# A mixture-of-experts tower: the gate rides in the routed row, the expert pass multiplies by it, and the gathers add rows into their target

## What is computed

```python
h = tok(x)                                       # softmax attention over patches
h = h + attn(layernorm(h), ...)                  # causal linear attention
h = h + ffn_moe(layernorm(h), ...)               # 8 experts, top 2
h = h + l1_attn(layernorm(h), ...)               # L1-normalised linear attention
h = h + bitlinear_ffn(layernorm(h), ...)         # quantised feed-forward

def ffn_moe(x, ...):
    routing = softmax(gelu(x @ w1 + b1) @ w2 + b2)
    topv, topi = top_k(routing, 2)
    sparse = one_hot(topi) * topv, summed over the two
    sparse = sparse / (sum(sparse) + 1e-8)       # the two gates of a token
    z = gelu(x @ down_w[e] + down_b[e])
    moe = sum over e of sparse[e] * (z @ up_w[e])
    return layer_norm(x + moe, gamma, beta)
```

## Time and profile before

| | |
|---|---|
| runs, us | 2739.93, 2738.08, 2753.07 |
| span of the profiled execution, us | 2748.1 |
| busy us: PE, DVE, ACT, POOL | 2290.8, 1996.1, 1551.7, 1004.0 |
| indirect transfers on POOL | 224 scatters, 241.3 us; 224 gathers, 229.3 us |
| first instruction of stage 3, of stage 4, us from the start | 1441.3, 1797.2 |

### The profile page before, as it was taken

One profiled execution on the slowest core, in us unless ns is written; L12 is line 12 of the kernel. 1 busy time (PEld: TensorE's weight loads), 2 busy tenths in 40 slices (PEclk: granted clock), 3 DMA queues, 4 the chain that ended last, 5 costly groups with the idle time before them and its releaser, 6 DMA issues. The chain is left out here.

```text
span 2748.1 us, 45420 instructions
## 1 busy us (share of the span) xinstructions
PE 2290.8 (83%) x14046; PEld 1660.5 (60%) x14047; DVE 1996.1 (73%) x5437; ACT 1551.7 (56%) x2693; POOL 1004.0 (37%) x1024
## 2 busy tenths in 40 slices
PE   8999999999996999999937999926778794666665
PEld 4444444444444888888827999925576684444443
DVE  5777777777763899999944444447698877899986
ACT  2444444444444788888734565536566551777776
POOL 1100100100000266566652444478787720344433
PEclk9999999999998999999958999957688886777776
DMA  2000000000002011111136777721111100000000
GB/s 57 0 18 13 0 18 13 0 9 1 0 0 90 16 53 51 51 52 52 51 111 221 257 252 258 238 77 50 46 48 43 46 9 22 21 26 21 26 26 26
DMA packets 69143, 162.81 MB, mean 59 GB/s; under 512 B 12977, under 2 KB 32342, under 8 KB 68702
## 3 DMA queue, kind: packets, MB, share of 16 engines
q1 hardware_dynamic: 39426, 94.27, 10.4%
q0 software_dynamic: 21504, 44.99, 5.8%
q10 hardware_dynamic: 8064, 21.68, 2.6%
HBM read 63.98 MB, written 63.88 MB: 47 GB/s over the span
## 5 line engine op out<-in xcount | busy, mean ns | idle before, releaser
L211 ACT ACTIVATE prob<-pscore 128x896 f32<-128x896 f32 x336 | 308.0, 917 | 423.9 <-PE pscore L293 423.9
L418 DVE TENSOR_REDUCE pmax<-ppre 112x1 f32<-112x512 f32 x656 | 424.5, 686 | 162.0 <-PE ppre L260 161.9
L307 PE MATMUL pout<-prob,xkey 128*64 128x448 f32 x1344 | 328.3, 567 | 0.4 <-ACT prob L211 0.4
L260 PE MATMUL ppre<-xh,yh 49*112 49x512 f32 x656 | 291.4, 446 | 7.8 <-DVE pmax L418 4.2
L723 POOL DMA_INDIRECT rows_in<-xr,idx x224 | 241.3, 1077 | 127.1 <-DVE idx L1249 69.5
L193 POOL CAST yh<-ynext 113x448 fp32r<-113x448 f32 x28 | 17.2, 614 | 667.5 <-DVE pmax L418 639.4
L260 PEld LDWEIGHTS ppre<-xh,yh 49*112 49x112 f32 x656 | 112.7, 172 | 239.8 <-issue 103.5
L1708 POOL DMA_INDIRECT yg<-rows_out,place x224 | 229.3, 1024 | 62.4 <-issue 62.1
L293 PE MATMUL pscore<-yh,xh 49*128 49x448 f32 x700 | 241.1, 422 | 0.4 <-DVE yh L438 0.4
L2223 POOL TENSOR_TENSOR yg<-y,gout 112x512 f32<-112x512 f32 x112 | 141.1, 1270 | 258.6 <-DVE y L2456 258.6
L1558 POOL TENSOR_TENSOR zl<-z,zh 128x448 fp32r<-128x448 f32 x126 | 144.5, 1147 | 218.3 <-ACT zh L1524 208.8
(11 more groups left out here) (388 smaller groups left out, 6558.0 us busy)
## 6 DMA issues: line engine op xcount, KB each, us to landing
wd<-down SPq DMA_DIRECT2D x63, 512.0 KB, 3.0
xb<-rows_in SPq DMA_DIRECT2D x63, 448.0 KB, 3.6
rows_out<-yb ACTq DMA_DIRECT2D x63, 336.0 KB, 3.1
out<-ho SPq DMA_DIRECT2D x28, 336.0 KB, 2.8
rows_in<-zero SPq DMA_DIRECT2D x15, 448.0 KB
rows_in<-xr,idx POOLq DMA_INDIRECT x224
yg<-rows_out,place POOLq DMA_INDIRECT x224
xkey<-in_xkey SPq DMA_DIRECT2D x4, 800.0 KB, 6.6
```

The costliest lines, as they stand in the source:

```text
L211: nc.scalar.activation(prob[j % 3][:, :, :], pscore[j % 2][:, :, 0:CH], ACT.Exp).then_inc(exped, 1)
L260: pe.matmul(out[:, :], yh1[rows, q * T:(q + 1) * T], xh[b % 2][rows, block * 512:(block + 1) * 512], start=True, stop=True, tile_position= ...
L307: mm = pe.matmul(pout[i * LO:(i + 1) * LO, 0:CH], xkey[b % 2][:, 2 * j + i, :], prob[j % 3][:, i, :], start=(j == 0), stop=(i == 1 and j = ...
L418: nc.vector.reduce_max(pmax[:, q, 2 * block + half:2 * block + half + 1], bank(u, depth), AX.X).then_inc(pre_max, 1)
```

## The change

Five things are moved or replaced.

- The rows of `rows_in`, `xr3`, `xb3` and the zero block grow from 256 to 260 floats (1024 to 1040 bytes). Column 256 carries the gate; columns 256 to 259 are cleared once. The table `gate3` of all tokens goes; two small buffers for one group stay.
- Stage 2: `share(r)` moves from the end of DVE's round to right behind `places(r)`. POOL's `scatter(r, k)` sends first the four sets with k = 0 and then, behind `factor`, the four with k = 1; ahead of each four it copies the gate of that k into column 256 of `xr3`, and ahead of the second copy it waits until the first four transfers have landed.
- Stage 3: a new `take_gate(t)` on DVE copies column 256 of the loaded rows to a small buffer, behind `take_y(t-2)`; `take_y` multiplies by it, four instructions of 192 columns in place of two copies of 384. `load(t)` on SP now also waits for the gate of tile t-2 (`gate_out`).
- Stage 4: the eight multiply-adds of `add_experts` go. The gathers target `acc3` itself and add to it (`compute_op=ALU.add`), first the four sets with k = 0, ahead of `factor`, then the four with k = 1, behind it and behind a wait for the first four. `acc3` has four buffers in place of three, ACT fills it one step earlier, and `yg3` goes.
- Waits that fed the removed instructions go (`half_out`, `acc_out`), others come (`gate_out`, `gate_in`, `xa_out` on POOL).

```diff
+ROW = 260
...
-            def scatter(r, tiles):
-
-                if 0 in tiles:
-                    pool.wait_ge(R["idx_out"], r + 1)
-                for q in tiles:
-                    for k in range(2):
-                        nc.gpsimd.indirect_dma_start(
-                            rows_in, bass.IndirectOffsetOnAxis(ap=idx[r % G3][:, 2 * q + k:2 * q + k + 1], axis=0),
-                            xr[r % G3][:, q, :], None).then_inc(scattered[r % G3], 16)
+            def scatter(r, k):
+
+                pool.wait_ge(R["gate_out"], r + 1)
+                pool.wait_ge(R["xr_ready"], r + 1)
+                if k:
+                    pool.wait_ge(scattered[r % G3], 16 * (2 * TPC * (r // G3) + TPC))
+                nc.gpsimd.tensor_copy(xr[r % G3][:, :, 256:257], gate[r % 2][:, :, k:k + 1]).then_inc(R["gate_in"], 1)
+                pool.wait_ge(R["gate_in"], 2 * r + k + 1)
+                pool.wait_ge(R["idx_out"], r + 1)
+                for q in range(TPC):
+                    nc.gpsimd.indirect_dma_start(
+                        rows_in, bass.IndirectOffsetOnAxis(ap=idx[r % G3][:, 2 * q + k:2 * q + k + 1], axis=0),
+                        xr[r % G3][:, q, :], None).then_inc(scattered[r % G3], 16)
...
                 if here(g - 3):
                     places(g - 3)
+                    share(g - 3)
...
-                if here(g - 3):
-                    share(g - 3)
...
                     sp.wait_ge(S["xtr_mm"], t - 1)
+                    sp.wait_ge(S["gate_out"], t - 1)
...
+            def take_gate(t, i):
+
+                dve.wait_ge(S["xtr_mm"], t + 1)
+                if not isinstance(t, int) or t >= 2:
+                    dve.wait_ge(S["y_out"], 2 * t - 2)
+                nc.vector.tensor_copy(gate[i][:], xb[i][:, :, 256:257]).then_inc(S["gate_out"], 1)
+
             def take_y(t, i, n):
 
+                dve.wait_ge(S["gate_out"], t + 1)
...
-                    nc.vector.tensor_copy(yb[i][:, 2 * pair:2 * pair + 2, :].rearrange("p q d -> p (q d)"),
-                                          py[i][:, pair, 0:2 * D]).then_inc(S["y_out"], 1)
+                    for q in (2 * pair, 2 * pair + 1):
+                        ts = nc.vector.tensor_scalar(yb[i][:, q, :], py[i][:, pair, (q % 2) * D:(q % 2 + 1) * D],
+                                                     gate[i][:, q, :], None, ALU.mult)
+                    ts.then_inc(S["y_out"], 1)
...
+            def gather_rows(g, k):
+
+                if k:
+                    pool.wait_ge(gathered[g % 2], 16 * (2 * TPC * (g // 2) + TPC))
+                else:
+                    pool.wait_ge(S["xa_out"], g + 1)
+                for q in range(TPC):
+                    c = g * 2 * TPC + 2 * q + k
+                    nc.gpsimd.indirect_dma_start(acc[g % 4][:, q, :], None, rows_out,
+                                                 bass.IndirectOffsetOnAxis(ap=place[:, c:c + 1], axis=0),
+                                                 compute_op=ALU.add).then_inc(gathered[g % 2], 16)
...
                 if here(s + 4):
-                    gather_rows(s + 4, (0, 1, 2))
+                    gather_rows(s + 4, 0)
                 if here(s + 3):
                     factor(s + 3)
                 if here(s + 4):
-                    gather_rows(s + 4, (3,))
+                    gather_rows(s + 4, 1)
...
-                for k in range(2):
-                    for q in range(TPC):
-                        st = nc.vector.scalar_tensor_tensor(acc[g % 3][:, q, :], yg[g % 2][:, q, k, :],
-                                                            gate[:, g * TPC + q, k:k + 1], acc[g % 3][:, q, :],
-                                                            ALU.mult, ALU.add)
```

More of the change, by code:

```diff
@@ L551, in _, with attend_route_phase @@
             inverse_root(nc, dve, link, rstd[:], var[:], root[:], dif[:])
-def attend_route_phase(nc, ins, h, bns, mean, rstd, minus, eye, held, gate, slot, shift, tile_e, tile_r, down,
+def attend_route_phase(nc, ins, h, bns, mean, rstd, minus, eye, held, slot, shift, tile_e, tile_r, down,
                        rows_in, scattered):
@@ L606, in attend_route_phase @@
         steps = sb("steps3", [T, 64])
-        zero = sb("zero3", [T, TPC * 256])
+        zero = sb("zero3", [T, TPC * ROW])
         agg3 = sb("agg3r", [T, TPC, 2])
         veps3 = sb("veps3r", [T, TPC])
-        xr = [sb(f"xr3_{i}", [T, TPC, 256]) for i in range(G3)]
+        xr = [sb(f"xr3_{i}", [T, TPC, ROW]) for i in range(G3)]
+        gate = [sb(f"gate3_{i}", [T, TPC, 2]) for i in range(2)]
         xrT = sb("xrT3", [KC, 2, CH])
@@ L694, in _ @@
                 pool.wait_ge(S["w_ready"], n + 1)
-            for n, (buf, value) in enumerate(((r1[KC:KC + 1], 1.0), (zero[:], 0.0))):
+            for n, (buf, value) in enumerate(((r1[KC:KC + 1], 1.0), (zero[:], 0.0), *((x[:, :, 256:ROW], 0.0) for x in xr))):
                 nc.gpsimd.memset(buf, value).then_inc(R["w_ready"], 1)
@@ L1233, in share @@
                 link(nc.vector.reciprocal(both[:], both[:]))
-                link(nc.vector.tensor_tensor(gate[:, r * TPC:(r + 1) * TPC, :], top[:, :, 0:2],
-                                             both[:].broadcast_to([T, TPC, 2]), ALU.mult))
+                if r >= 2:
+                    dve.wait_ge(R["gate_in"], 2 * r - 2)
+                nc.vector.tensor_tensor(gate[r % 2][:], top[:, :, 0:2], both[:].broadcast_to([T, TPC, 2]),
+                                        ALU.mult).then_inc(R["gate_out"], 1)
             def take_rank(r):
@@ L1358, in expert_phases @@
             route_sems = []
-            attend_route_phase(nc, ins, h, bns, mean, rstd, minus, eye, route_sems, gate, slot, shift, tile_e, tile_r,
+            attend_route_phase(nc, ins, h, bns, mean, rstd, minus, eye, route_sems, slot, shift, tile_e, tile_r,
                                down, rows_in, scattered)
@@ L1362, in expert_phases @@
                        held + route_sems)
-        linear_attention_phase(nc, ins, h, bns, rstd, minus, eye, gate, place, rows_out)
+        linear_attention_phase(nc, ins, h, bns, rstd, minus, eye, place, rows_out)
 def tile_phase(nc, ins, eye, down, slot, place, shift, tile_e, tile_r, rows_in, rows_out, held):
@@ L1372, in tile_phase @@
         downb = sb("downb", [128, 2 * E])
-        xb = [sb(f"xb3_{i}", [T, TPC, 256]) for i in range(2)]
+        xb = [sb(f"xb3_{i}", [T, TPC, ROW]) for i in range(2)]
+        gate = [sb(f"gate3b_{i}", [T, TPC, 1]) for i in range(2)]
         xth = [sb(f"xth3b_{i}", [128, 2, CH], F32R) for i in range(2)]
@@ L1603, in tile @@
                     take_y(t - 1, 1 - i, n + i - 1)
+                if not last:
+                    take_gate(t + 1, 1 - i)
                 if isinstance(t, int) and t == 2:
@@ L1613, in _ @@
             take_low(0, 0)
+            take_gate(0, 0)
             split_low(0)
@@ L1617, in _, with linear_attention_phase @@
             take_y(NTILE - 1, (NTILE - 1) % 2, (NTILE - 1) // 2)
-def linear_attention_phase(nc, ins, h, bns, rstd, minus, eye, gate, place, rows_out):
+def linear_attention_phase(nc, ins, h, bns, rstd, minus, eye, place, rows_out):
     RB = D - 128
@@ L1632, in linear_attention_phase @@
         mhalf = sb("mhalf_3", [T, TPC])
-        yg = [sb(f"yg3_{i}", [T, TPC, 2, D]) for i in range(2)]
-        acc = [sb(f"acc3_{i}", [T, TPC, D]) for i in range(3)]
+        acc = [sb(f"acc3_{i}", [T, TPC, D]) for i in range(4)]
         yf = sb("yf3", [T, TPC, D])
@@ L1680, in linear_attention_phase @@
         NW = 5
-        LEAD = 4
+        LEAD = 5
         def here(g):
@@ L1942, in _ @@
                     magnitudes(s, c, 0)
-                if here(s + 4):
-                    rows_entered(s + 4)
+                if here(s + 5):
+                    rows_entered(s + 5)
                 if s >= 0:
```

39 lines of the change are left out of this document (12 added, 27 removed).

## The result

The changed kernel takes 2886.81 us (median of four runs, 2885.72 to 2890.23) against 2739.01 us (median of four, 2736.62 to 2753.07), 148 us or 5.4% more by the medians. The ratio of the runs on record is 1.0517, 95% interval 1.0494 to 1.0539. The kernel is slower, as forecast, but by 148 us and not by 36, and outside the range.

The account below looks back on a forecast made before the run. PE was taken to bound stages 2 and 3, POOL most of stage 4. Terms 8 + 3 + 0 + 2 - 3 - 3 - 2 + 31 = +36 on 2739.93 gave 2776 us, range 2724 to 2860.

Parts of the forecast that it names:

- The direction and the bound: Whole kernel and stage 4: slower by over 0.5% at chance 0.55; POOL bounds about 19 of stage 4's steps.
- -6 for all of stage 4 without the price: Stage 4's other terms: steady steps -3 us, turns of images -3, first landing +2, after the last group -2.
- The price of an adding gather: Stage 4, POOL: an adding gather costs 0.15 us more than a plain 0.93; +31 us, 0 to 190 at the bounds.
- 204p: Stage 4: cost of p more per adding gather, from 19 x 8p in steps, 7 x 4p at turns, 24p at start.
- Rival C: Stage 4: adding lists each row's target for reading too, +0.47 to +0.93 us a gather; 2841 to 2935 us, chance 0.15.
- The wait: Stage 4: second four gathers wait for the first four to land, mostly covered by `factor`; 0.1 us a step.
- The relief: Stage 4: without DVE's multiply-adds POOL's `factor` and gathers run faster, 0.25 us a step; with the wait, -3 us.
- Stage 3's zero: Stage 3: PE stays the bound, the later load still lands with 0.3 us of slack; 0 us.
- rival D: Stage 3: loads come 0.5 us late, 59 times; +30 us on top of any case, chance about 0.15 on its own.
- `share`: Stage 2: `share` ahead of `gate_in` delays each of 24 rounds by 0.35 us; +8 us, 0 to 14.
- The end: Stage 2's last three groups pay uncovered landings and copies, POOL ending at 1436.8 against SP's 1433.6; +3 us, 0 to 7.

## Why the prediction was wrong

**The direction and the bound were right.** POOL bounds the steady steps of stage 4: 0.6 us off POOL shortened the step by 0.66, and without the eight multiply-adds on DVE stage 4 took 449.0 us against 450.1. DVE is not free there, though: the two runs in which its additions got cheaper had stage 4 shorter by 4 to 6 us. The prediction had -6 for all of stage 4 without the price; it is -1.

**The price of an adding gather was mis-sized, and its reason was wrong.** This is the step that failed. The price was taken as 0.15 above plain, inside bounds of 0 and 0.93; it is 0.57 by the medians (1.512 against 0.936). The sum's 204p would be 116 us for the 31 forecast; 102 were lost. Its parts came out near: 82 us in the 19 steady steps (152p would be 87) and 21 at the turns (28p would be 16). Nothing was lost at the start, for which it had 24p, because the first steps are among the 19. The choice went by the nearest row because "the price goes by the rows listed": the run with 56 rows shows that it hardly goes by rows, for plain gathers either. A plain row had nothing to tell on an instruction of another sort, and a wide bound was then treated as if its low end were likely. Rival C had the size (0.47 to 0.93) but the wrong mechanism, that each row is listed twice: then adding 56 rows would have cost about 0.29 us more than gathering them, and it cost 0.53. Why an adding gather has this fixed price stays open. By the rule of the Trainium skill in "Collectives: The Full Stack", section "The bandwidth ceiling: the fold count and why AG ≠ RS ≠ AR", told there for the sums of collectives, a summed chunk takes two read descriptors, and rival C would hold. The trace agrees in the sign alone: the queue of POOL's transfers holds more packets (then MB and share of the engines' time), first without the adding, then with it,

```profile
q0 software_dynamic: 21504, 45.39, 5.7%
```

```profile
q0 software_dynamic: 39424, 45.39, 8.3%
```

80 more for each of the 224 gathers with no more bytes, but POOL's time did not follow the rows.

**The wait was mis-sized, and so was what covers it.** It was taken as 0.1 us a step, since `factor` with 1.95 us covers a plain landing, and 0.25 of relief was set against it. The wait costs 0.70. With adding gathers `factor` covers less, its second instruction being 0.62 shorter, which pays most of that back. The relief was to come from DVE's multiply-adds; without them, and with plain gathers, the instruction was no shorter (1.68). Those plain steps took 13.41 us against 13.51 (mean of the 19 steady ones), near the forecast of 0.15 less; what they gained lies in the gathers, 0.99 us in the mean against 1.02 to 1.04. What shortens `factor` beside adding gathers stays open.

**Stage 3's zero was rival D.** The load's issue was worked out rightly, 1.24 us behind the transposes' start and 1.39 in the trace. (The old issue at 1607.70 did not stand "beside the end of the transposes": those that it waits for had ended 3.6 us earlier. The sum doesn't use that.) With the landing of before, 3.6 us in the median, the slack of 0.3 would nearly have held: behind the first four tiles, where the 5.2 us stands, loads landed in 3.2 to 3.9 us and one in 4.4, and of the changed kernel's loads that miss the store PE waited for one of 31. What failed is that the landing was taken from loads that go out 1.6 us or more ahead of ACT's store. At the new time they go out together at every second tile; those loads landed in 4.6 us, and PE waited 0.7 for each. The step that put it at 0 did not look at what else is issued then.

**Stage 2 was near.** `share`: +8 forecast, 9 to 12 measured, by the path described. The copies and waits in the steady rounds are hidden, as said. The end: +3 forecast, 7.7 measured. POOL's last issue ended at 1438.71 + 0.94 = 1439.65, forecast 1436.8; the third landing, 3.4 us for the 1.8 taken, is about half of that. And the step that failed set POOL's issue against SP's transfers as landed (1433.6), leaving out that POOL's last rows have to land as well: with 2 us for that, an estimate from the two waits of 2.08 and 1.78, it is 1441.7 against 1433.6, 8 us.

**The range.** C with D on top comes to 2841 + 30 = 2871 and more by the text's own numbers, but the range stopped at 2860. The two don't exclude each other, and both sizes came.

## What to carry to other kernels

Price an instruction of a new sort by running it, and until then let the range reach the upper bound: a near relative's row says little. Moving work off an engine pays where that engine is late: here 0.6 us less on POOL shortened the step by 0.66, while 2.8 us a step less on DVE, with the new order, gave 1 us in a whole stage. A load that is moved to a later time must be set against the other transfers that go out then, and not only against its usual landing; copying the one column out early bought the whole stage back.

## What the runs showed of the hardware

POOL's time to issue an indirect gather is nearly a constant per instruction: 0.956 us for 56 rows and 0.975 for 112. Adding in the transfer raises it to 1.487 and 1.567. The landing, counted from the start of the issue, goes from 2.5 and 2.6 us to 3.1 and 3.5, so most of what it grows by is the longer issue.

The first POOL instruction behind an adding gather is recorded at 0.76 us in place of 0.22 for the same 112x4 addition, but it costs no more: its record begins while the gather's still runs. In the step shown the gather before it is recorded from 2002.66 for 1.71 us, to 2004.37, and the addition ends at 2004.61, 0.24 behind that.

A load of 455 KB that goes out 0.08 us behind a store of 336 KB lands in 4.6 us in the median, and in 3.8 when it goes out 0.3 to 1.1 us ahead of it (28 and 30 loads of the changed kernel).
